# A graph and mixture-of-experts kernel on one core: one gather in every second group moved from GpSimd to row loads by the sync engine

## What is computed

```python
def gnn(features, src, dst, w, W, b):
    msgs = features[src] * w[:, None]
    agg = segment_sum(msgs, dst, num_segments=12500)
    return agg @ W.T + b
x = x + gnn(layernorm(x), src, dst, edge_weight, W, b)
x = x + expert_ffn(layernorm(x))      # top 1 of 8, capacity 1.25 * T / 8
```

## Time and profile before

| | |
|---|---|
| time, median of 3 runs | 2926.6 us (2921.68 to 2930.18) |
| span of the profiled execution, first to last instruction | 2424.0 us |
| time less span | 502.6 us |
| busy share of the span: PE, DVE, ACT, POOL | 75%, 45%, 45%, 74% |
| mean granted TensorE clock | 0.851 |
| gathers on POOL | 1,666 |

### The profile page before, as it was taken

One profiled execution on the slowest core, in us unless ns is written; L12 is line 12 of the kernel. 1 busy time (PEld: TensorE's weight loads), 2 busy tenths in 40 slices (PEclk: granted clock), 3 DMA queues, 4 the chain that ended last, 5 costly groups with the idle time before them and its releaser, 6 DMA issues.

```text
span 2424.0 us, 33618 instructions
## 1 busy us (share of the span) xinstructions
PE 1825.1 (75%) x9798; PEld 1181.3 (49%) x9798; DVE 1087.4 (45%) x5806; ACT 1088.6 (45%) x2563; POOL 1792.8 (74%) x1873
## 2 busy tenths in 40 slices
PE   3444566666888878788778778778788887887699
PEld 1222243334656555455445445445454554554598
DVE  8877433334555443443443443443444444443232
ACT  6777233333555544344344344344444444454243
POOL 7777777777777777777777777777777777775673
PEclk9999955557999988787887888888988988898899
DMA  7776333345555554445345454545454455555467
GB/s 241 228 230 196 105 108 112 111 133 173 159 158 160 170 179 116 152 147 160 117 152 155 116 192 125 181 119 161 146 195 152 119 194 157 188 157 168 149 245 290
DMA packets 139869, 394.79 MB, mean 163 GB/s; under 512 B 36197, under 2 KB 62821, under 8 KB 129046
## 3 DMA queue, kind: packets, MB, share of 16 engines
q0 software_dynamic: 89712, 244.29, 33.9%
q1 hardware_dynamic: 46276, 135.53, 16.1%
q10 hardware_dynamic: 3698, 12.80, 1.5%
HBM read 496.75 MB, written 40.76 MB: 222 GB/s over the span
## 4 chain that ended last, share of the span: by engine, by line
POOL 68%; issue 22%; PE 7%; DVE 2%; DMA 1%; ACT 1%; SPq 0%; POOLq 0%; ACTq 0%; DVEq 0%
POOL msg L650 64%; POOL rows_by_expert L676 4%; PE ps L1003 3%; PE ps L991 3%; DMA hin<-rows_by_expert 0%; DMA msg<-normed,src_sb 0%; PE ps L891 0%; PE ps L973 0%; ACT hmid L808 0%; SPq L608 0%; DVE aggT L1079 0%; DVE aggT L1075 0%; PE ps L965 0%; DVE wsl L1172 0%; PE ps L900 0%
## 5 line engine op out<-in xcount | busy, mean ns | idle before, releaser
L650 POOL DMA_INDIRECT msg<-normed,src_sb x1462 | 1398.1, 956 | 445.5 <-issue 445.5
L891 PE MATMUL ps<-msg,onehot 128*32 128x256 f32 x3332 | 428.5, 498 | 384.6 <-DMA msg<-normed,src_sb 303.7
L1216 DVE TENSOR_TENSOR aggT<-aggT,ps 128x192 f32 x294 | 104.1, 354 | 903.7 <-PE ps L900 896.9
L770 ACT COPY pairs<-ps 128x256 f32<-128x256 f32 x294 | 112.6, 383 | 730.5 <-PE ps L891 720.7
L891 PEld LDWEIGHTS ps<-msg,onehot 128*32 128x32 f32 x3332 | 137.7, 127 | 565.6 <-DMA msg<-normed,src_sb 366.1
L1003 PE MATMUL ps<-wsl,hmid 128*128 128x256 f32 x1680 | 393.8, 388 | 1.4 <-ACT hmid L808 1.4
L973 PE MATMUL ps<-wsl,hTf 128*128 128x512 f32 x680 | 379.9, 711 | 0.8 <-ACT hTf L797 0.8
L1003 PEld LDWEIGHTS ps<-wsl,hmid 128*128 128x128 f32 x1680 | 316.2, 193 | 68.9 <-issue 28.9
L900 PE MATMUL ps<-shift,pairs 128*128 128x96 f32 x1176 | 238.1, 335 | 94.4 <-ACT pairs L770 94.4
L808 ACT ACTIVATE hmid<-ps,wsl 128x128 f32<-128x128 f32 x840 | 229.6, 381 | 120.7 <-PE ps L991 74.0
L900 PEld LDWEIGHTS ps<-shift,pairs 128*128 128x128 f32 x1176 | 192.3, 231 | 160.5 <-ACT pairs L770 156.7
(11 more groups left out here) (134 smaller groups left out, 2252.4 us busy)
## 6 DMA issues: line engine op xcount, KB each, us to landing
wsl<-in_wsecond SPq DMA_DIRECT2D x105, 1152.0 KB
wsl<-in_wfirst SPq DMA_DIRECT2D x105, 1028.0 KB
msg<-normed,src_sb POOLq DMA_INDIRECT x1462
xrow<-in_x SPq DMA_DIRECT2D x97, 128.0 KB, 2.3
wsl<-in_x SPq DMA_DIRECT2D x24, 512.0 KB, 4.0
normed<-wsl ACTq DMA_DIRECT2D x24, 512.0 KB, 3.2
hin<-rows_by_expert SPq DMA_DIRECT2D x89, 130.0 KB, 2.7
msg<-in_x,src_sb POOLq DMA_INDIRECT x204
```

The source lines that it names most:

```text
L650: pool.indirect_dma_start(out=msg[:, m + j, :], out_offset=None, in_=x if t < RAW else ln_dram, in_offset=bass.IndirectOffsetOnAxis(ap=src ...
L770: nc.scalar.copy(pairs[:, t % 2, :], ps[:, t % 2, 0:D]).then_inc(s_pair, 1)
L891: last = nc.tensor.matmul(ps[h * QWIN:(h + 1) * QWIN, t % 2, 0:D], onehot[:, j, :], msg[:, j, :], start=i == 0, stop=i == QUARTERS[q][h] - 1)
```

## The change

In the groups 14, 16, ..., 92 (40 of them) the last column of the group's first tile (t = 42, 48, ..., 276) is left out of POOL's gathers. SP loads it into a buffer of its own, `side` (three of them), as 128 transfers of one row, each with the row's number in a register. SP first brings the column's 128 indices into one partition of `side_i`, and reads them into registers 16 at a time. The eight batches of a column are placed at the `mm` events of tiles t-7 to t-2. Before the first, SP waits until the buffer's last user has been summed. PE waits for the 128 rows before it sums the tile.

```diff
+SIDE_FROM, SIDE_STEP, SIDE_LAST = 14, 2, 92
+SIDE_BUFS = 3
+SIDE_BATCH = 16
+SIDE_AHEAD = 7
...
+        def gathered(t):
+            return SUBS[t % 3] - (1 if t in SIDE_OF else 0)
...
+            def side_indices(k):
+                u = k % SIDE_BUFS
+                sp.dma_start(side_i[:, u, :], side_t[:, k * P:(k + 1) * P]).then_inc(s_sidei[u], 16)
+
+            def side_rows(k, b):
+                u = k % SIDE_BUFS
+                if b == 0:
+                    sp.wait_ge(s_sidei[u], 16 * (k // SIDE_BUFS + 1))
+                    if k >= SIDE_BUFS:
+                        before = SIDE[k - SIDE_BUFS]
+                        sp.wait_ge(s_mm[before % RING], summed(before))
+                first = b * SIDE_BATCH
+                _, nodes = nc.values_load_multi_w_load_instructions(
+                    side_i[:, u, first:first + SIDE_BATCH], engines=[mybir.EngineType.SP], min_val=0, max_val=N - 1,
+                    skip_runtime_bounds_check_because="the source of an edge is a node")
+                for i, node in enumerate(nodes):
+                    p = first + i
+                    sp.dma_start(side[p:p + 1, u, :], ln_dram[bass.ds(node, 1), :]).then_inc(s_side[u], 16)
+                if b == BATCHES_SIDE - 1 and k + 2 < len(SIDE):
+                    side_indices(k + 2)
...
             for kind, *key in EVENTS:
-                if kind == "rb" and key[0] + 2 < NT:
+                if kind == "mm":
+                    for k, b in side_at.get(key[0], ()):
+                        side_rows(k, b)
+                elif kind == "rb" and key[0] + 2 < NT:
                     load_x(key[0] + 2)
...
-                for j in range(SUBS[q]):
+                for j in range(gathered(t)):
...
+                if t in SIDE_OF:
+                    k = SIDE_OF[t]
+                    pe.wait_ge(s_side[k % SIDE_BUFS], 16 * P * (k // SIDE_BUFS + 1))
...
-    nc = bacc.Bacc("TRN2", target_bir_lowering=False, num_devices=1)
+    nc = bacc.Bacc("TRN2", target_bir_lowering=False, num_devices=1, dynamic_dma_scratch_size=8192)
```

More of the change, by code:

```diff
@@ L57, in layout_of, with side_groups @@
     return dict(tiles=tiles, group=group, subs=subs, quarters=quarters, columns=columns, queue=queue)
+def side_groups():
+    return range(SIDE_FROM, SIDE_LAST + 1, SIDE_STEP)
 def visits_after(tiles, experts, n):
@@ L251, in schedule_of, with gnn_moe_kernel @@
     return dict(events=order, full=full, visits=visits, batches=batches, after=after, turned=turned)
-def gnn_moe_kernel(nc, x, src_t, dst_t, w_t, w_gnn, b_gnn, gate_w, gate_b, wfirst, wsecond, consts, pads, out,
-                   sizes, F):
+def gnn_moe_kernel(nc, x, src_t, dst_t, w_t, w_gnn, b_gnn, gate_w, gate_b, wfirst, wsecond, consts, pads,
+                   side_t, out, sizes, F):
     N, D = x.shape
@@ L273, in gnn_moe_kernel @@
     OWN = {v: min(v, NT - 1) for v in range(V)}
+    SIDE = [3 * g for g in side_groups()]
+    SIDE_OF = {t: k for k, t in enumerate(SIDE)}
     SEEN0 = E8 * QUEUE + P
@@ L329, in gnn_moe_kernel @@
         tbuf = sb("tbuf", [P, D])
+        side = sb("side", [P, SIDE_BUFS, D])
+        side_i = sb("side_i", [1, SIDE_BUFS, P], I32)
         ids, fin = src_sb[:, 0:V], wgt[:, 0:V]
@@ L411, in gnn_moe_kernel @@
         s_msg = [sem(f"s_msg{u}") for u in range(RING)]
+        s_side = [sem(f"s_side{u}") for u in range(SIDE_BUFS)]
+        s_sidei = [sem(f"s_sidei{u}") for u in range(SIDE_BUFS)]
         s_rawmv, s_rawsd, s_rawsc, s_norm = sem("s_rawmv"), sem("s_rawsd"), sem("s_rawsc"), sem("s_norm")
@@ L479, in third, with message @@
             return g, q, t % RING, (t % RING) * SUBS[0]
+        def gathered(t):
+            return SUBS[t % 3] - (1 if t in SIDE_OF else 0)
         def arrived(t):
-            return 16 * sum(SUBS[k % 3] for k in range(t % RING, t + 1, RING))
+            return 16 * sum(gathered(k) for k in range(t % RING, t + 1, RING))
+        def message(t, j):
+            if t in SIDE_OF and j == SUBS[t % 3] - 1:
+                return side[:, SIDE_OF[t] % SIDE_BUFS, :]
+            return msg[:, (t % RING) * SUBS[0] + j, :]
         def summed(t):
@@ L608, in pad_queues @@
                     sp.dma_start(hbuf[bass.ds(row, PADS), :], pads).then_inc(s_pads, 16)
+            def side_indices(k):
[17 more added lines that the diff above has]
+                    side_indices(k + 2)
+            BATCHES_SIDE = P // SIDE_BATCH
+            side_at = {}
+            for k, t in enumerate(SIDE):
+                for b in range(BATCHES_SIDE):
+                    side_at.setdefault(t - SIDE_AHEAD + 3 * SIDE_STEP * b // BATCHES_SIDE, []).append((k, b))
+            side_indices(0)
+            side_indices(1)
             for kind, *key in EVENTS:
-                if kind == "rb" and key[0] + 2 < NT:
+                if kind == "mm":
+                    for k, b in side_at.get(key[0], ()):
+                        side_rows(k, b)
+                elif kind == "rb" and key[0] + 2 < NT:
                     load_x(key[0] + 2)
@@ L889, in aggregate @@
                         if i < QUARTERS[q][h]:
-                            j = m + QOFF[q][h] - OFF[q] + i
-                            last = nc.tensor.matmul(ps[h * QWIN:(h + 1) * QWIN, t % 2, 0:D], onehot[:, j, :],
-                                                    msg[:, j, :], start=i == 0, stop=i == QUARTERS[q][h] - 1)
+                            j = QOFF[q][h] - OFF[q] + i
+                            last = nc.tensor.matmul(ps[h * QWIN:(h + 1) * QWIN, t % 2, 0:D], onehot[:, m + j, :],
+                                                    message(t, j), start=i == 0, stop=i == QUARTERS[q][h] - 1)
                             if i == QUARTERS[q][h] - 1:
@@ L1465 @@
     pads[:, X_ID] = NOBODY
+    side_columns = [g * z["group"] + z["subs"][0] - 1 for g in side_groups()]
+    side_t = by_tile(inputs["src"], 0)[:, side_columns].T.reshape(1, -1)
     def rows(a):
```

1 line of the change is left out of this document (added).

## The result

| | before | after |
|---|---|---|
| time, median of 4 runs | 2924.14 us (2912.84 to 2930.18) | 4177.78 us (4170.08 to 4181.75) |
| ratio, 95% interval | | 1.4293 (1.4259 to 1.4326) |
| span of the profiled execution | 2424.0 us | 4173.6 us |

The change makes the kernel 43% slower.

A forecast was written before the change was run, and what follows sets the result against it. POOL's gathers were taken to bound the kernel, with SP becoming the bound after the change. Start 236 + columns 3828 + old work 230 + landing and sum 5 + end 304 = span 4603; plus 502.6 makes 5106 us, range 3800 to 6060.

The forecast's parts named there:

- A column on SP, C = 95.7 us: SP's 128 row issues (67.5 us) plus register loads (28.2 us) per side column; SP's earlier loads, the old work, come on top.
- size has made no difference so far: SP's loads to SBUF: issue time taken as independent of transfer size, so a one-row issue was priced at 333 ns.
- 502.6 us outside the span: Whole kernel: the runs' median lay this far above the profiled span, and it was added to the forecast span of 4603 us.
- The start, 236 us: Before the first column: SP can begin its row loads once all normed rows are stored, at 236 us.
- From tile 276 to the end, 304 us: After the last side column: the old 322.5 us, less an estimated 18 for gathers POOL does ahead.
- the old waits: SP's waits for other engines, the four largest 1845 us of 2424, were to go to about nothing.
- PE's wait ends last by `side`: Sign in the changed profile: PE's idle time before L891 should end by `side`, not `msg`.
- The hidden one: Rival: SP's column work fits beside POOL's pair of groups, C below 40, full 50 us gained, time 2877; chance 0.08.
- Cheap loads, issue as in L583: Rival on SP: row issues at full price, register batches at 2.1 us a column, C 69.6, time 4062 us; chance 0.15.
- cheap issue, dear loads: Rival on SP: row issues at 80 ns, register loads 28.2 us a column, C 63.7, time 3826 us; chance 0.13.
- The queue holds SP: Rival: SP must wait for each row to land, a column 256 us, time over 11,000 us; chance 0.03.
- Scratch: Rival: POOL stays the bound and the halved descriptor space or PE eats the gain, no change; chance 0.01.

The follow-up runs named there:

- m1: Separate kernel, nine phases of 64 SP row loads with POOL idle or busy: register-address rows took 30.5 us idle, 98.7 beside 64 gathers, 30.5 beside ACT's 1 MB loads.
- e0: The kernel before, unchanged, run and profiled again: 2948.99 us, ratio 1.000, span 2941.3 us.
- e2: The changed kernel with each side column as one load of 128 adjacent rows (wrong rows), no register loads: 2912.21 us, ratio 0.987 to the kernel before.
- e3: The changed kernel with the 128 one-row issues at fixed addresses (wrong rows), no register work: 3000.76 us, ratio 1.017 to the kernel before.
- e1: The kernel before with only the descriptor space halved to 8,192 bytes of each partition: 2953.18 us, ratio 1.0027.
- m2: Second separate kernel of phases, varying POOL's work and the issuing engine: 64 register-address rows by SP took 35.6 us idle, 30.3 beside plain transfers, 111.9 beside unbroken gathers.
- m3: Third separate kernel of phases, with memset breaks among POOL's gathers: 64 rows by SP took 33.1 us with long breaks after six gathers, 111.5 with none.

## Why the prediction was right, and where its numbers were not

The direction, the mechanism and the range held; the forecast of 5106 us was 22% above the time. Term by term, against the span of 4173.6 us:

- **A column on SP, C = 95.7 us, and 5.9 of old work in a pair: 101.6.** The first row was issued at 277.5 us, the fortieth column began at 3660.5: 86.7 us for each, old work included. From the first row to the sum of tile 276 it is 3752.2 - 277.5 = 3475 us where the sum had 3828 + 230 + 5 = 4063, so 588 us too large. Its parts are off in both directions. A clean row is 0.41 us, not 0.53, by an issue of 228 ns, not 333: "size has made no difference so far" didn't hold for the step from 128 rows to one, though in m1 16 rows (316 ns) cost nearly what 128 do. The 16 registers are 0.98 us, not 3.5: the three-register load on DVE was no guide to a load of 16 on SP. Clean, that makes 61 + 6 = 67 us. The other 20 are hold-ups, and the prediction had no such term: it priced an instruction of SP the same whatever POOL does.
- **502.6 us outside the span.** There are 1.8, in the changed kernel and in the old one (e0). This was the median of one kind of execution less the span of another. It should have been a warning: a fifth of the time lay outside the span and nothing in the profile said what it was.
- **The start, 236 us.** 277.5; the normed rows were stored 39 us later than in the quick profile.
- **From tile 276 to the end, 304 us.** (4173.6 - 3752.2) = 421 us; the unchanged kernel in e0 has 425. It is the longer executions' delay, on work that the change doesn't touch.

The sum closes: 5106 - 588 - 501 + 41 + 117 = 4175, the time of the profiled run. The errors cancelled in part, and the ratio shows what that hid: 5106 over 2926.6 is 1.74, the measured one is 1.43.

That the time fell into the range was luck in part. The direction and the bound don't hang on it: even a clean column, 61 + 6 us, is more than a pair of groups. But put the clean prices, the measured start and end and no hold-ups into the same sum, and it gives 277 + 40 x 67 + 421 + 2 = 3380 us, below the range's lower end of 3800. The register load priced at three and a half times its cost, the issue at one and a half times, and the 501 us that weren't there more than made up for a term of some 800 us (40 x 20) that the prediction didn't have.

**What the steps said.** POOL's end as the bound, the chain moving to SP, the old waits vanishing up to tile 276 and POOL waiting for PE: all as written. "PE's wait ends last by `side`" was half right; the largest of its waits ends through ACT by `hin`. The old work on SP was to take 5.9 us a pair and takes 7.3, hold-ups included. A pair was to last some 98 us and lasted 86; the 98 is a slip, the forecast's own terms make 101.6. The granted clock fell where PE starved, as written: 0.70 with PE busy for 43% of the time from 277 to 3752 us, where it had been 0.87 with PE busy for 81%. PE's busy time was 38 us a pair, no bound.

**The rivals.** The hidden one priced the gain at 50 us; e2, which has the cover, gained 38. Its condition, C below 40, was right in kind: e3, whose clean column is 37 us, should then just have been hidden on an undisturbed chip; beside the hold-ups it wasn't. "Cheap loads, issue as in L583" (4062 us) and "cheap issue, dear loads" (3826) come closer to the time than the forecast does, and in truth both terms were cheaper than forecast. They don't add up to the hidden case, since even at 0.41 us a row 128 of them are 53 us, more than a pair. "The queue holds SP" was out: landing times never showed in the pitch of clean rows. "Scratch": 0.1 to 0.4% by the interval of e1, which is small beside the loss either way.

The Trainium skill's rule that the time a sequencer takes to start a transfer is usually small beside the transfer ("DMA: Bandwidth & Descriptors", "Issuing engines are not separate DMA queues") is no guide for many small ones: in m1 the last row of 1 KB had landed 1.2 us after its issue began, against 0.41 us of SP for each row, yet 128 of them in a row made SP the bound. The Trainium skill's page "Runtime: NRT & Kernel Launch" ("Instruction fetch mechanics") has some 200 ns for each register in a TENSOR_LOAD, even in bulk; there the loads are from HBM. Here, from SBUF, 16 together took 0.98 us, 61 ns each, while a single one took 265.

**Without hold-ups**, on a chip like the fourth, the changed kernel would by the clean terms have a span of about 775 + 40 x 61 = 3215 us beside 2424. That it loses there too is an estimate and not measured.

## What to carry to other kernels

An engine that only waits is not free: price the instructions that one unit of moved work needs there, and compare with the time between two units of the engine that is relieved; here 384 sequencer instructions and 8 register loads stood against 1.25 us of POOL. Anything that shares an in-order queue with such a burst (here weight, row and x loads) can come late even where the burst itself would fit, and spreading it thinner did not rescue it. And when the time of the runs and the span of the profile differ by more than a few microseconds, find out why before a number of that profile is used: run the unchanged kernel again and compare the stage lengths.

## What the runs showed of the hardware that I had not expected

- SP's instructions, register-only ones included, are held up about 0.7 us at a time while POOL issues gathers of 128 rows 1.25 us apart: 64 rows in 98.7 and 111.9 us for 30.5. Memsets on POOL, plain transfers by POOL and 409 GB/s of loads by ACT do nothing of the kind. It begins some 1 to 12 us into a run of gathers on SP, lasts 11 to 13 us beyond the last of 64 or 76 gathers, and is nearly gone where gathers are 1.5 us apart on the mean (m1, m2, m3). ACT's issues are held in the same way from 17 us on (m2).
- In the same executions the signals from PE to ACT and DVE come some 1 to 7 us late in a run of gathers, which makes the kernel before 54.6 us a pair where POOL needs 45. That both have one cause is likely and not shown, though the issues that ACT makes are held as SP's are.
- The same program took 2945 to 2950 us on three chips and 2430 on a fourth, and on the fourth no hold-up could be found. What differs is open.
- An issue of one row by SP is 228 ns, of 16 rows 316, of 128 rows 333 (m1); a row with its register work 0.41 us; 16 registers in one load 0.98 us.
